# When ScalarE takes the side banks of a state-space scan, and a third buffer for turned values in attention

## The chip, the cores and the metric

The kernel runs on one core of one Trainium2 chip. A core has a matrix engine (TensorE, PE in the profile), a vector engine (VectorE, DVE), an activation engine (ScalarE, ACT), a general engine (GpSimd, POOL), and a sync engine (SyncE, SP) that here only issues DMAs. The metric is the device time of one execution in microseconds.

## The reference, cut to what matters

The input is `x` of 16 sequences x 1024 positions x 256. Three things are computed, each added to its input:

```
xz = layernorm(x) @ in_w.T;  x_, z = halves of xz (512 wide each)
u  = silu(conv4(x_) + conv_b)                        # causal, 4 taps
dt_in, B, C = u @ x_proj.T                           # 64, 16, 16 wide
delta = softplus(dt_in @ dt_w.T + dt_b)
h = h * exp(delta * A) + (delta * u) * B             # step by step, 512 channels x 16 states
y = (sum over states of h * C + u * D) * silu(z)
x = x + y @ out_w.T
n = layernorm(x)
attention over the 16 sequences at each place (16 heads of 16, causal),
then 8 experts of width 1024, two chosen per token, 320 x 16 rows at most each
x = x + n + attention + experts
```

All of it is float32.

## The kernel before, in words

There are four stages, one after the other: `mamba_stage` (state space), `attention_stage`, `routing_stage`, `expert_stage`. The change touches the first two. Every engine runs a list of its own, written out by hand; semaphores join the lists.

**State space.** The work is cut into 32 blocks: 16 sequences, each in two halves of 512 positions. A block is 32 units (`UNITS`): two passes over halves of the channels, each of 16 states. A unit has two chunks of 128 channels, so a block has 64 positions `v`, and position `v` belongs to unit `v // 2`. "Position" below always means this. Channels lie on the partitions and the 512 places along the row, so one VectorE instruction scans 128 channels of one state over 512 places.

For each position ScalarE makes `decay = exp(delta * A)` into one of two PSUM banks (L521). VectorE scans it (L639), which needs `decay` and GpSimd's `dbu = du * B` (L373). The decay of position `v` overwrites that of `v - 2`, so it waits for that scan. Per unit the state is multiplied by C: 13 of the 32 units (`POOL_UNITS`: remainder 1 or 3 by five) on GpSimd (L382), the other 19 on VectorE (L621, one scan later, with C spread over the partitions by a TensorE pick, L751). TensorE adds the products over the states with a unit matrix (`sum_unit`, L767). It does so two units later, for the first state of a pass three units later, after two products with the skip diagonal (L760). At positions 4 and 5 (second pass of the block before) and 36 and 37 (first pass) VectorE multiplies the finished sum by the gate (L575).

**The side work.** Beside scanning one block the kernel prepares the next one: turning the normed rows (`xnT`), the input projection (`x`), the convolution (`conv`), the B/C/dt projection (`dbl`), `dt`, and the gate branch (`z`). It also finishes the block before (`out`, the output projection). The list `SIDE` says at which position TensorE does which piece of 0.9 us or so. Three PSUM banks (`SIDE_BANKS`) take these uses in turn. The use at index n can be filled when the one at n - 3 has been emptied. Who empties a bank, and at which position after the last piece:

- `xnT`, `x`, `dbl`: one ScalarE copy, 1 position later (`take`, called from `prepare`);
- `dt`: ScalarE takes it 1 position later (two instructions), `softplus_exp` 2 later, `softplus_ln` 3 later, and VectorE adds the two parts of delta 4 later (L613);
- `conv` and `z`: ScalarE takes them 2 positions later (tanh, and for conv a scaled copy), VectorE's `silu` (L567) is 3 later;
- `out`: VectorE's `add_residual` (L581), 1 later.

`prepare` runs on ScalarE after the decay of its position; `finishing` and `preparation` run on VectorE after the scan of theirs. On TensorE the even piece of a unit comes before that unit's `sum_unit`, the odd piece after it, and the pick last. Each list is strict in its order, so an engine that waits in one of these steps holds everything behind it.

Derived places: `REST_AT`, `MIDDLE_AT` and `LOW_AT` split C into three bf16 parts (VectorE, ScalarE twice, VectorE); `STORE_ROWS_AT` is the unit at which SyncE stores the B and C rows; `DU_AT` are the two units at which GpSimd makes `du = delta * u` (`du_part`, L365) for the next block; `STATS_AT` and `NORMALISE_AT` place the statistics and the norm. The first block is prepared ahead of the loop. The last block prepares nothing.

**Attention.** 64 items of 16 places each pass through a pipeline of steps; the constants (`KDIAG`, `VTURN`, ...) say how many steps after its start an item reaches an operation. For an item VectorE turns the values into `vtr` (`turn_values`, L1225) at lag 10, GpSimd spreads them with 8 DMAs into the block-diagonal `vbd` (`place_values`, L1066) at lag 11, and TensorE multiplies by them at lag 13. `vtr` and `vbd` both have two buffers. VectorE's list of a step ends with `statistics`, `turn_values`, `statistics_2`; GpSimd's is `inverse_deviation_2`, `inverse_deviation`, `place_values`.

## Time and profile before

| | us |
|---|---|
| three runs | 7350.12, 7351.43, 7352.06 (median 7351.43) |
| profiled execution, whole | 7356.11 |
| profiled execution, span of the core | 7354.4 |
| busy: PE / DVE / ACT / POOL | 6352.4 / 4186.9 / 3217.9 / 5285.3 |
| share of the span | 86% / 57% / 44% / 72% |

The page's slices show three kinds of stretch. Up to about 4100 us (state space) PE, DVE and POOL are all at 8 or 9 tenths. From there to about 4950 us (attention) PE is at 9. After a short stretch in which nearly only POOL works (routing), the experts run from about 5300 us to the end with PE at 9 and the others low. The core's whole time is the sum of these stages, so what a change in a stage brings is read inside it.

### The profile page before, as it was taken

Reading aid. Unit: us, or ns where it says so; the run is one execution under the profiler, and the core shown is the slowest. Engines: PE = TensorE matmul, PEld = TensorE weight load, DVE = VectorE, ACT = ScalarE, POOL = GpSimd, SP = SyncE. Lnnn points to the kernel's source line nnn. Section 1 sums busy time; section 2 is a strip of 40 time slices with the busy share of each in tenths; the row PEclk is TensorE's granted clock in tenths of the full one; section 3 lists DMA queues with packets and bytes.
Section 4 is the critical chain, followed back from the end, with each engine's and each line's share of the span. In section 5 each row is a group of like instructions: output and inputs, shape, how many; then the busy total and the mean of one; then the engine's idle time right before and its main releaser. Section 6 shows DMA issues by size and latency. Waiting matters only on the chain. (4 is left out here: it accounts for less than half of the span.)

```text
span 7354.4 us, 88415 instructions
## 1 busy us (share of the span) xinstructions
PE 6352.4 (86%) x25412; PEld 3944.7 (54%) x25412; DVE 4186.9 (57%) x5063; ACT 3217.9 (44%) x5905; POOL 5285.3 (72%) x4089
## 2 busy tenths in 40 slices
PE   7989989898989989898888799970089999999999
PEld 3433434334434434343343577760078888888888
DVE  6988888888888888888888465661000000000000
ACT  5555555555555555555555466650022222222222
POOL 6988888888888888888889666636744444444444
PEclk9999999999999999999999999985599999999999
DMA  3333333333333333333333233330055555555554
GB/s 90 112 104 108 103 112 104 111 104 110 103 104 111 104 111 99 112 104 110 104 108 107 69 100 108 109 114 1 1 184 181 176 181 176 177 179 174 178 155 133
DMA packets 469314, 869.97 MB, mean 118 GB/s; under 512 B 72818, under 2 KB 241268, under 8 KB 434352
## 3 DMA queue, kind: packets, MB, share of 16 engines
q1 hardware_dynamic: 353616, 509.92, 23.2%
q0 software_dynamic: 115296, 355.56, 16.0%
q8 instruction: 147, 2.41, 0.1%
q14 instruction: 255, 2.09, 0.1%
HBM read 766.65 MB, written 88.88 MB: 116 GB/s over the span
## 5 line engine op out<-in xcount | busy, mean ns | idle before, releaser
L373 POOL TENSOR_TENSOR m_dbu<-m_du,m_bb 128x1024 f32<-128x1024 f32 x1024 | 2390.7, 2355 | 135.8 <-DVE m_h L639 135.2
L767 PE MATMUL m_y_bank<-m_prod,m_ident 128*128 128x512 f32 x4096 | 1995.0, 614 | 170.9 <-POOL m_prod L382 169.9
L521 ACT ACTIVATE m_decay<-m_delta,m_a_neg 128x512 f32<-128x512 f32 x2048 | 1402.8, 692 | 1121.9 <-DVE m_h L639 1112.9
L767 PEld LDWEIGHTS m_y_bank<-m_prod,m_ident 128*128 128x128 f32 x4096 | 787.0, 196 | 1163.9 <-issue 883.3
L639 DVE TENSOR_TENSOR_SCAN m_h<-m_decay,m_h_end,m_dbu 128x512 f32<-128x512 f32 x1024 | 1268.3, 1270 | 168.2 <-ACT m_decay L521 152.8
L639 DVE TENSOR_TENSOR_SCAN m_h<-m_decay,m_dbu 128x512 f32<-128x512 f32 x1024 | 1208.0, 1211 | 234.8 <-ACT m_decay L521 175.0
L1717 DVE TENSOR_SCALAR e_ye<-e_ybank,e_listing 128x256 f32<-128x256 f32 x270 | 118.3, 480 | 1887.1 <-PE e_ybank L1752 1887.1
L382 POOL TENSOR_TENSOR m_prod<-m_h,m_cb 128x1024 f32<-128x1024 f32 x416 | 978.5, 2352 | 247.2 <-DVE m_h L639 198.9
L1752 PE MATMUL e_ybank<-e_w,e_a 128*128 128x256 f32 x4320 | 968.5, 382 | 35.1 <-ACT e_a L1703 35.1
L1703 ACT ACTIVATE e_a<-e_ubank 128x512 f32<-128x512 f32 x540 | 322.4, 597 | 1543.4 <-PE e_ubank L1743 1541.1
L1743 PE MATMUL e_ubank<-e_xT,e_w 128*128 128x256 f32 x4320 | 956.0, 379 | 1.3 <-ACT e_xT L1694 1.3
L1752 PEld LDWEIGHTS e_ybank<-e_w,e_a 128*128 128x128 f32 x4320 | 809.6, 190 | 171.9 <-ACT e_a L1703 67.3
L1743 PEld LDWEIGHTS e_ubank<-e_xT,e_w 128*128 128x128 f32 x4320 | 821.8, 190 | 113.6 <-issue 1.6
L1647 POOL DMA_INDIRECT e_w<-in_w,weight_row x270 | 258.3, 957 | 847.3 <-PE e_ybank L1752 800.5
L621 DVE TENSOR_TENSOR m_prod<-m_h,m_c_bank 128x1024 f32<-128x1024 f32 x608 | 728.2, 1198 | 93.1 <-PE m_c_bank L751 79.4
L725 PE MATMUL m_side<-m_xnT,m_w_in 128*128 128x512 f32 x1024 | 546.8, 634 | 19.8 <-ACT m_xnT L440 19.8
L1664 POOL DMA_INDIRECT out<-e_ye,e_token x270 | 430.1, 1593 | 113.7 <-issue 81.3
L730 PE MATMUL m_side<-m_xpad,m_tap_diag 128*128 128x512 f32 x1024 | 505.8, 592 | 0.0
L1729 PE MATMUL e_tbank<-e_ident,e_xe 128*128 128x128 f32 x540 | 81.5, 274 | 368.4 <-DMA e_xe<-n,e_token 368.4
L751 PE MATMUL m_c_bank<-m_c_parts,m_pick 80*128 80x512 bf16 x608 | 239.2, 393 | 164.1 <-DVE m_prod L621 164.0
L1481 POOL DMA_INDIRECT info<-r_entry,r_slot_of x256 | 250.9, 980 | 134.7 <-issue 80.4
L1655 POOL DMA_INDIRECT e_xe<-n,e_token x270 | 284.1, 1052 | 82.5 <-issue 82.5
(207 smaller groups left out, 6705.5 us busy)
## 6 DMA issues: line engine op xcount, KB each, us to landing
m_bb<-rows_bc SPq DMA_DIRECT2D x1024, 256.0 KB, 3.5
m_cb<-rows_bc SPq DMA_DIRECT2D x416, 256.0 KB, 3.4
m_xin<-in_x SPq DMA_DIRECT2D x32, 512.0 KB, 5.3
m_xres<-in_x SPq DMA_DIRECT2D x32, 512.0 KB, 5.3
x<-m_xres SPq DMA_DIRECT2D x32, 512.0 KB, 4.9
a_xa<-x SPq DMA_DIRECT2D x64, 256.0 KB, 2.9
a_xr<-x SPq DMA_DIRECT2D x64, 256.0 KB, 3.1
out<-a_out_base SPq DMA_DIRECT2D x64, 256.0 KB, 3.1
```

Of the source, the lines that this page charges most:

```text
L373: nc.gpsimd.tensor_tensor(dbu[:, slot], du[:, q[1], p * PC:(p + 1) * PC], bb[:, slot].unsqueeze(1).to_broadcast([P, PC, T]), ALU.mult).the ...
L382: nc.gpsimd.tensor_tensor(prod[:, slot], h[:, slot], cb[:, C_BUFFER[k]].unsqueeze(1).to_broadcast([P, PC, T]), ALU.mult).then_inc(prod_by_ ...
L521: nc.scalar.activation(decay[:, cc], delta[:, r, c], ACT.Exp, scale=a_neg[:, c, n:n + 1]).then_inc(decay_done, 1)
L621: nc.vector.tensor_tensor(prod[:, slot], h[:, slot], c_bank[:].unsqueeze(1).to_broadcast([P, PC, T]), ALU.mult).then_inc(prod_by_vector, 1)
L639: nc.vector.tensor_tensor_scan(h[:, slot, cc], decay[:, cc], dbu[:, slot, cc], h_end[:, u, cc:cc + 1] if r else 0.0, ALU.mult, ALU.add).th ...
L725: ins = nc.tensor.matmul(bank, w_in[:, piece, col:col + P], xnT[:, piece], start=(piece == 0), stop=final)
L730: ins = nc.tensor.matmul(bank, tap_diag[:, i, piece], xpad[:, i, piece:piece + T], start=(piece == 0), stop=final)
L767: ins = nc.tensor.matmul(y_bank[:, cc], ident[:], prod[:, slot, cc], start=False, stop=(n == NS - 1))
L1664: nc.gpsimd.indirect_dma_start(out, bass.IndirectOffsetOnAxis(ap=token[:, col:col + 1], axis=0), ye[:, n % Y_RING, j], None, compute_op=AL ...
L1703: nc.scalar.activation(a[:, n % 2, g * PER_U:(g + 1) * PER_U], ubank[:, (n * UG + g) % U_RING], ACT.Gelu).then_inc(u_taken, 1)
L1743: ins = nc.tensor.matmul(ubank[:, (n * UG + g) % U_RING, i], w1[:, r, k, c * P:(c + 1) * P], xT[:, n % 2, k], start=(k == 0), stop=(k == K ...
L1752: ins = nc.tensor.matmul(ybank[:, n % 2, j], a[:, n % 2, c, j * P:(j + 1) * P], w2[:, r, c], start=(c == 0), stop=(c == FC - 1))
```

## The change

ScalarE's takes move from 1 to 3 positions after the last piece (`TAKE`), and from 2 to 4 for conv and z (`TAKE_SILU`). `softplus_exp` and `softplus_ln` move with them (to 4 and 5), VectorE's `silu` goes from 3 to 4 and delta from 4 to 5. In `SIDE` the x uses begin one position later, `dt` and `out` one later, `z` where it was, so a rest before `z` is gone. `MIDDLE_AT` is three positions after `REST_AT` and `LOW_AT` is at the same position as `MIDDLE_AT`. In attention `vtr` has three buffers, and `turn_values` waits for the placing of the item three before instead of two before.

```diff
-    SIDE = [("xnT", 0, 1), ("xnT", 1, 1), REST, ("x", 0, KH), ("x", 1, KH), REST, ("conv", 0, TAPS), ("x", 2, KH),
+    SIDE = [("xnT", 0, 1), ("xnT", 1, 1), REST, REST, ("x", 0, KH), ("x", 1, KH), ("conv", 0, TAPS), ("x", 2, KH),
             ("conv", 1, TAPS), ("x", 3, KH), ("conv", 2, TAPS), REST, ("conv", 3, TAPS), REST, REST, ("dbl", 0, CH),
-            REST, REST, ("dt", 0, 1), ("out", 0, 4), ("dt", 1, 1), ("out", 1, 4), ("dt", 2, 1), REST, ("dt", 3, 1),
-            REST, REST, ("z", 0, KH), ("z", 1, KH), ("z", 2, KH), ("z", 3, KH), REST, REST, REST, REST]
+            REST, REST, REST, ("dt", 0, 1), ("out", 0, 4), ("dt", 1, 1), ("out", 1, 4), ("dt", 2, 1), REST, ("dt", 3, 1),
+            REST, ("z", 0, KH), ("z", 1, KH), ("z", 2, KH), ("z", 3, KH), REST, REST, REST, REST]
+    TAKE, TAKE_SILU = 3, 4
...
-    assert position_of["z", CH - 1] + 3 < POSITIONS
+    assert position_of["z", CH - 1] + TAKE_SILU < POSITIONS
     STATS_AT = position_of["dt", 0] + 3
     NORMALISE_AT = STATS_AT + 8
-    REST_AT = position_of["dbl", 0] + 2
-    MIDDLE_AT = REST_AT + 1
-    LOW_AT = MIDDLE_AT + 1
-    STORE_ROWS_AT = (position_of["dbl", 0] + 2) // PC
-    DU_AT = ((position_of["dt", 1] + 4) // PC + 3, (position_of["dt", 3] + 4) // PC + 1)
+    REST_AT = position_of["dbl", 0] + TAKE
+    MIDDLE_AT = REST_AT + 3
+    LOW_AT = MIDDLE_AT
+    STORE_ROWS_AT = (position_of["dbl", 0] + 2 + TAKE) // PC
+    DU_AT = ((position_of["dt", 1] + TAKE + 2) // PC + 3, (position_of["dt", 3] + TAKE + 2) // PC + 1)
...
-                if v - 2 in filled_at and filled_at[v - 2][0] in SILU_KINDS:
-                    take(q, *filled_at[v - 2])
-                if v - 1 in filled_at and filled_at[v - 1] in prep_uses and filled_at[v - 1][0] not in SILU_KINDS:
-                    take(q, *filled_at[v - 1])
-                if v - 2 in filled_at and filled_at[v - 2][0] == "dt":
-                    softplus_exp(q, filled_at[v - 2][1])
-                if v - 3 in filled_at and filled_at[v - 3][0] == "dt":
-                    softplus_ln(q, filled_at[v - 3][1])
+                silu_of, plain = filled_at.get(v - TAKE_SILU), filled_at.get(v - TAKE)
+                exp_of, ln_of = filled_at.get(v - TAKE - 1), filled_at.get(v - TAKE - 2)
+                if silu_of and silu_of[0] in SILU_KINDS:
+                    take(q, *silu_of)
+                if plain in prep_uses and plain[0] not in SILU_KINDS:
+                    take(q, *plain)
+                if exp_of and exp_of[0] == "dt":
+                    softplus_exp(q, exp_of[1])
+                if ln_of and ln_of[0] == "dt":
+                    softplus_ln(q, ln_of[1])
...
-                if v - 3 in filled_at and filled_at[v - 3][0] in SILU_KINDS:
-                    silu(p, *filled_at[v - 3])
-                if v - 4 in filled_at and filled_at[v - 4][0] == "dt":
-                    c = filled_at[v - 4][1]
+                silu_of, dt_of = filled_at.get(v - TAKE_SILU), filled_at.get(v - TAKE - 2)
+                if silu_of and silu_of[0] in SILU_KINDS:
+                    silu(p, *silu_of)
+                if dt_of and dt_of[0] == "dt":
+                    c = dt_of[1]
...
-    X_RING, RES_RING, SIDE_BANKS = 4, 3, 4
+    X_RING, RES_RING, SIDE_BANKS, TURN_RING = 4, 3, 4, 3
...
-        vtr = sb("vtr", [P, 2, 2, GL, HD])
+        vtr = sb("vtr", [P, TURN_RING, 2, GL, HD])
...
-                    nc.gpsimd.dma_start(vbd[rows, k % 2, g], vtr[rows, k % 2, g % 2]).then_inc(v_placed[k % 2], 16)
+                    nc.gpsimd.dma_start(vbd[rows, k % 2, g], vtr[rows, k % TURN_RING, g % 2]).then_inc(v_placed[k % 2], 16)
...
-                wait(dve, v_placed[k % 2], turns(k - 2, 2, KV))
-                nc.vector.transpose(vtr[:, k % 2].rearrange("p g l d -> p l g d"),
+                if k >= TURN_RING:
+                    wait(dve, v_placed[(k - TURN_RING) % 2], turns(k - TURN_RING, 2, KV))
+                nc.vector.transpose(vtr[:, k % TURN_RING].rearrange("p g l d -> p l g d"),
```

By the lists, this is where some steps stand (position before, position after): take of `x` 0: 5, 8; of `dbl`: 35, 37; `rest`: 36, 37; `middle`: 37, 40; `low`: 38, 40; last piece of `dt` 0 to 3: 37, 42, 47, 49 before and 38, 43, 48, 50 after; take of `dt` 2: 48, 51; deltas 0 to 3: 41, 46, 51, 53 before and 43, 48, 53, 55 after; takes of `z` 0 to 3: 55, 57, 59, 61 before and 57, 59, 61, 63 after; `du_part`: units 26 and 27 before, 27 and 28 after. Between the emptying of a bank and the first piece of the next use there were at least 2 positions before; now it is 1 for `out` 1 (freed by delta 0 at 43, filled from 44), `z` 1 (53, 54), `z` 2 (55, 56) and `z` 3 (57, 58).

## Rows read from the trace of the kernel before

**Rows 1.** Windows: length, busy us (instructions) by engine, clock, DMA share, GB/s.

```profile
300.00:4000.00 3700.00, 3319.41 (x8030) 1474.42 (x8031) 3227.83 (x3243) 2029.16 (x3659) 3242.34 (x1492) 0.95 0.36 107
...
4250.00:4800.00 550.00, 508.89 (x5177) 431.63 (x5176) 332.53 (x787) 376.93 (x754) 348.67 (x935) 0.97 0.36 105
...
5400.00:7200.00 1800.00, 1769.49 (x8290) 1532.98 (x8289) 106.87 (x244) 401.92 (x732) 877.99 (x732) 1.00 0.57 175
```

**Rows 2.** Waits of DVE, 300 to 4200 us: total, times, longest.

```profile
DVE m_h L639 <- ACT m_decay L521: 310.9, 275, 3.3
DVE m_prod L621 <- PE m_c_bank L751: 79.4, 43, 5.9
DVE m_h L639 <- POOL m_prod L382: 34.7, 11, 4.1
```

**Rows 3.** Waits of ACT, the same stretch.

```profile
ACT m_sp_r L470 <- PE m_side L738: 172.5, 58, 4.8
ACT m_tanh L460 <- PE m_side L725: 165.1, 86, 4.9
ACT m_tanh L457 <- PE m_side L730: 100.7, 87, 3.9
...
ACT m_c_middle L500 <- DVE m_side L602: 97.6, 29, 3.4
```

**Rows 4.** Windows of two blocks: scan 6, gate 36, scan 44, next scan 6.

```profile
2097.84:2153.10 55.26, 53.30 (x127) 23.00 (x127) 48.81 (x47) 29.18 (x59) 50.65 (x23) 1.00 0.33 99
2153.10:2171.86 18.76, 17.05 (x43) 8.58 (x44) 16.13 (x24) 11.16 (x21) 11.44 (x6) 0.82 0.32 103
2171.86:2221.96 50.10, 41.89 (x107) 18.34 (x105) 43.80 (x43) 30.39 (x61) 46.42 (x24) 0.97 0.39 121
2221.96:2277.30 55.34, 53.34 (x127) 23.00 (x127) 50.76 (x45) 27.75 (x44) 52.56 (x24) 1.00 0.33 98
2277.30:2295.32 18.02, 16.96 (x42) 8.89 (x43) 16.44 (x24) 10.65 (x17) 11.41 (x5) 0.82 0.37 110
2295.32:2350.26 54.94, 44.15 (x107) 18.87 (x106) 44.63 (x43) 29.87 (x52) 48.73 (x25) 0.94 0.38 111
```

**Rows 5.** Two groups of DVE, whole run: busy us, mean ns, idle before.

```profile
L621 DVE TENSOR_TENSOR m_prod<-m_h,m_c_bank 128x1024 f32<-128x1024 f32 x608 | 728.2, 1198 | 93.1 <-PE m_c_bank L751 79.4 <-issue 12.4 <-DVE m_h L639 0.7
...
L613 DVE TENSOR_TENSOR m_delta<-m_side,m_sp_r 128x512 f32<-128x512 f32 x128 | 85.9, 671 | 7.9 <-ACT m_side L484 7.9
```

**Rows 6.** Timeline of POOL, second half of a block: start, us.

```profile
2295.48 2.36 POOL L382 TENSOR_TENSOR m_prod<-m_h,m_cb 128x1024 f32<-128x1024 f32 x1 [2.46 <-DVE m_h L639]
...
2311.00 2.35 POOL L373 TENSOR_TENSOR m_dbu<-m_du,m_bb 128x1024 f32<-128x1024 f32 x1
2316.78 2.35 POOL L365 TENSOR_TENSOR m_du<-m_delta,m_xc 128x1024 f32<-128x1024 f32 x1 [3.42 <-DVE m_delta L613]
...
2328.33 2.34 POOL L382 TENSOR_TENSOR m_prod<-m_h,m_cb 128x1024 f32<-128x1024 f32 x1
...
2338.26 2.35 POOL L382 TENSOR_TENSOR m_prod<-m_h,m_cb 128x1024 f32<-128x1024 f32 x1 [0.65 <-DVE m_h L639]
```

**Rows 7.** Timeline of DVE and PE, the same block and one before.

```profile
2192.91 2.33 DVE L639 TENSOR_TENSOR_SCAN m_h<-m_decay,m_dbu 128x512 f32<-128x512 f32 x2
...
2323.80 2.95 PE L767 MATMUL m_y_bank<-m_prod,m_ident 128*128 128x512 f32 x4 [2.86 <-POOL m_prod L382]
...
2341.24 3.45 DVE L639 TENSOR_TENSOR_SCAN m_h<-m_decay,m_dbu 128x512 f32<-128x512 f32 x3 [3.14 <-POOL m_prod L382]
```

**Rows 8.** Attention, steps 16 to 58 (42 steps): window.

```profile
4311.40:4825.60 514.20, 469.47 (x4813) 397.93 (x4812) 311.50 (x736) 345.46 (x696) 316.52 (x841) 0.97 0.36 106
```

**Rows 9.** Attention, waits of DVE, 4250 to 4860 us.

```profile
DVE a_vtr L1225 <- DMA a_vbd<-a_vtr: 216.1, 51, 7.8
```

**Rows 10.** Attention, timeline of one step.

```profile
4510.29 3.91 POOL L1066 DMA_DIRECT2D a_vbd<-a_vtr  x8 [0.32 <-POOL a_shift_n L1052]
...
4517.37 0.71 DVE L1225 STREAM_TRANSPOSE a_vtr<-a_vT 128x512 f32<-128x512 f32 x1 [6.08 <-DMA a_vbd<-a_vtr]
```

## The prediction

> **What bounds the kernel now.** I read the windows by stage first, then who waits for whom inside a stage, then windows and timelines of two neighbouring blocks, since the takes move by positions inside a block. The reader should see three stages with three limits. In the experts PE is busy 98% of the stretch and the change touches nothing there. In attention PE has 92 or 93%. In the state space PE, POOL and DVE stand at 90, 88 and 87% [rows 1]: none is the bound alone, each waits for the others in turn. So I look for which list ends last in which part of a block.
>
> DVE's largest wait there is for ScalarE's decay, 310.9 us in 275 pieces; the wait for the picked C comes far behind [rows 2]. ScalarE is busy for only 55% of the stretch [rows 1], so it isn't slow, it is held: its takes wait for PE (172.5, 165.1, 100.7 us) and its middle part of C for DVE (97.6 us) [rows 3]. A decay queued behind such a take comes late. That is what the change goes at. The question is what ends next where the decay no longer does.
>
> Cut a block at scan 6, gate 36 and scan 44, and the two blocks of [rows 4] give A = 55.26 and 55.34 us, B = 18.76 and 18.02, C = 50.10 and 54.94, together 252.42, or 126.2 per block. In A PE is busy for 53.3 of 55.3 us at a granted clock of 1.00 (2.4 GHz): A belongs to PE, whatever ScalarE does. In B the clock is 0.82, part of the time at the 1.2 GHz level, and PE and DVE each have some idle time. In C DVE has 6.3 and 10.3 us of idle time, PE 8 to 11, and POOL 3.7 to 6.2 [rows 4].
>
> **Part 1, the takes in A (gain 0.8 us per block).** The piece of dt 0 leaves A for B and the last piece of x 1, which stood ahead of the skip products, now comes after them. A piece is about 0.86 us at full clock, half of a sum's 1.9 less its tail [rows 7]. PE's unbroken stretch in A is 53.3 less the dt piece (1.1) plus 0.86, so 53.1 us. DVE can't come right behind: its product of unit 15 needs a pick that PE issues 6.4 us before the end of that stretch (two sums of 1.9 us less tail, three pieces, a pick), and from there it has its product (1.2, [rows 5]), a silu (0.7), four scans at 1.14 (two in 2.33 us, less the 1.2 of one, [rows 7]) and another product (1.1) to gate 36. That is 46.8 + 7.7 = 54.5 us against 55.3. The ends: 53.2 (PE alone) and 56 (a piece late by one).
>
> **Part 2, B (gain 2.0).** The wait of 3.4 us per block for the middle part goes: DVE makes `rest` at 37, and ScalarE asks for it at 40. The take of dt 0 moves from one to three positions behind PE. DVE's own work in B is 16.13 and 16.44 us [rows 4] and nothing else is later than it, so B comes to 16.4, against 18.4 on the mean. Ends: 0 (PE's skip products start no earlier) and 2.3.
>
> **Part 3, C (gain 3.8).** DVE's own work is 43.8 and 44.6 us [rows 4]; for both I take 44.7. What is late next is POOL. From the product of unit 21 (start 2295.48) to the end of that of unit 31 (2340.61) it has 45.1 us, of which 3.42 go to `du` waiting for delta 3 and 0.65 to a scan [rows 6]. In the new order the product of unit 26 comes ahead of the second `du`, so the wait for delta 3 (now two positions later, and `du` one unit later) is filled: 41.1 us of work without a break. DVE, without its stops, has 19 scans at 1.14, five products at 1.2 and seven short steps like the delta at 0.67 [rows 5, 7] from scan 44 to product 30: 32.4 us. PE picks C for that product behind the sum of unit 28, and POOL ends the product of unit 28 today at 2330.67, 35.2 us after that of unit 21 began [rows 6]; without the wait for delta 3 that is 31.8. A sum of 1.9 and a pick of 0.4 follow: 34.1, so DVE waits 1.7 us. The clock adds to it. After an idle time of 2.86 us PE needed 2.95 us for a sum instead of 1.9 [rows 7], and the new idle time in front of the sum of unit 28 is about as long; another sum after 2.4 us was not slowed, so I take 0.8 of a possible 1.7. C is then 44.7 + 1.7 + 0.8 = 47.2 for the first block. In the second the loop's turn adds the 3.1 us in front of its first scan [rows 7], which the view gives to POOL but which stands at every second block start; it stays: 50.3. The mean gain is (2.9 + 4.6)/2 = 3.8. Ends: 1.0 (the wait for the pick grows to 4) and 6.5 (all of DVE's idle time but the loop's turn).
>
> The Trainium skill speaks against this part. "TensorE: Matmul & The Clock Gate", section "HAM oscillation — how this bites in real kernels", says that a matmul loop which waits between its bursts is put back to half rate at each wait. The trace agrees for one such wait, 2.95 us for a sum behind 2.86 us of idleness. If it held at every block, C would lose the full 1.7 us, 0.9 more than I take, and the time would be 28 us higher.
>
> **Part 4, the banks (0, ends 0 and 8 us per block).** Four uses now have one position between the emptying and the first piece: out 1, z 1, z 2, z 3. By the sum of Part 3 PE comes to z 2 and z 3 after DVE's delta 3 and silu, with 0.4 us to spare or to wait; z 1 waits up to 0.3 us for delta 2. PE has idle time in C [rows 4], which hides these. If that cover were gone, each costs up to a position, 2 us. ScalarE's extra work at one position is 1.9 us at most (end of dt 2 and take of dt 3 at 53), against scans, a product and a delta on DVE; it doesn't hold the decay. SyncE's store of the rows comes a unit later and holds the load of B for unit 23, which POOL reads only after scan 39: nothing.
>
> Per block 0.8 + 2.0 + 3.8 = 6.6 us. 31 of the 32 blocks prepare a next one: 205 us.
>
> **Part 5, the third buffer (gain 38 us).** Steps of attention take 514.2/42 = 12.2 us [rows 8]. DVE waits 216 us for the DMAs that spread the turned values [rows 9]. That wait closes a loop one step long: turn, second statistics, POOL's two inverse deviations, eight DMA issues of 3.91 us together, landing 3.2 us after the last issue (4514.20 to 4517.37), turn again [rows 10]. It takes a whole step, and PE loses 514.2 - 469.5 = 44.7 us over these 42 steps [rows 8]. With three buffers the placing waited for is two steps old, the loop has a step to spare, and PE's own work remains: 11.2 us per step. Over some 50 steps the most to be had is 1.06 x 50 = 53 us; the least is 0, since PE has 91% without it. I take 0.75 of 1.06 per step, 38 us, because ScalarE's copies and the bank order also cost PE short waits.
>
> **Sum.** 7356.1 - 205 - 38 = 7113 for an execution like the profiled one. The median of the three runs lies 4.7 us below that execution, so 7108.
>
> **Rivals.** (a) All of DVE's wait for the decay comes back: POOL and PE follow at once. For it: DVE is idle for 5 to 6 us of A and 6 to 10 us of C [rows 4]. Against: PE fills A without a gap. 311 + 50 give 6995. (b) C is POOL's: the idle time of DVE there turns into waits for picks and for POOL, and only A and B gain. For it: POOL has 46.4 of 50.1 us in C [rows 4]. Against: it loses 3.4 us to `du` that the new order fills. 31 x 2.8 = 87, with half of attention 19: 7245. (c) Slower: the banks of Part 4. PE would reach out 1, z 1, z 2 and z 3 before DVE has freed them, each time wait a position, and carry the lag through the next A, where it has no slack. Four waits of 2 us are 8.0 against the gain of 6.6, 1.4 x 31 = 43 us more, with nothing gained in attention: 7394. It decides from the point where the four waits together pass 6.6 us. For it: one position of slack where there were two to three. Against: PE is behind DVE in these units by the sum of Part 3. (d) The change does nothing measurable, since ScalarE's held time moves to another wait of the same length: 7351.
>
> **How the numbers follow.** A measurement of this kernel tells 0.2% (15 us) from no change. Forecast 0.57 (7050 to 7190), (a) 0.10, (b) 0.22, (c) 0.07, (d) 0.04. Range: the upper end 7285 takes in (b) with nothing from attention (7264); the lower end 7000 the far ends of Parts 3 and 5 (2.7 x 31 = 84 and 15 us lower: 7009); (a), (c) and (d) are left out. Faster 0.90, same 0.03, slower 0.07.
>
> **What would show it.** ScalarE's waits for PE's side banks near nothing, and for `middle` gone. DVE's wait for the decay from 311 us to below 60, its wait for picks up from 79 to over 120. A about 54.5, B 16.4, C 47 to 50 us in windows cut in the same way. GpSimd's wait for delta 3 under 1 us. In attention no DVE wait for the placing, steps of 11.4 us. The prediction is wrong if DVE waits as long as before under another name, if C stays over 49 on the mean, or if PE waits for banks at z 1 to z 3.

## The result, and the profile after

The changed kernel takes 7055.84 us (median of four runs, 7053.51 to 7057.36) against 7350.89 (7350.12 to 7352.06) for the kernel before on the same chip: a ratio of 0.9598, 95% interval 0.9582 to 0.9615. Its profiled execution took 7057.36 us, with a span of 7055.6. The forecast was 7108 with a range of 7000 to 7285. The direction and the range held, and the mechanism in the main; the saving was 295 us where I had worked out 243.

The two profiled executions lie 299 us apart. Of these the state space gives 215 (its last instruction ends at 3887.8 instead of 4103.3 us) and attention 83 (755.9 instead of 839.0 us long). Routing and the experts did not move.

The windows by stage of the kernel after, with the columns of [rows 1]. The second lies wholly in attention.

```profile
300.00:3800.00 3500.00, 3241.02 (x8039) 1451.05 (x8038) 3216.62 (x3250) 2049.89 (x3665) 3242.93 (x1495) 0.97 0.37 113
4030.00:4500.00 470.00, 470.00 (x5077) 407.29 (x5072) 340.30 (x772) 378.23 (x735) 358.12 (x926) 1.00 0.42 121
5100.00:6900.00 1800.00, 1769.49 (x8290) 1533.07 (x8289) 106.84 (x244) 401.90 (x731) 878.19 (x731) 1.00 0.58 175
```

The same 8030 or so matmuls of the state space now fit into 3500 us instead of 3700 [rows 1]: PE, DVE and POOL stand at 93, 92 and 93%. In attention PE is busy for 470.00 of 470.00 us at a clock of 1.00. PE's time in the experts, 1769.49 us, is that of before to a hundredth.

The waits of DVE in the state space, 300 to 3900 us (total, times, longest), against [rows 2]:

```profile
DVE m_prod L625 <- PE m_c_bank L755: 180.8, 78, 5.6
DVE m_prod L625 <- issue: 47.2, 29, 4.6
```

The 310.9 us for ScalarE's decay are gone to the last one. What is late next is the pick of C, 180.8 instead of 79.4 us. Taken together, DVE stands idle for 283 of 3500 us where it stood for 472 of 3700 [rows 1], with the same work: of the 311 us removed some 120 came back under other names.

The waits of ScalarE, same stretch, against [rows 3]:

```profile
ACT m_decay L524 <- DVE m_h L643: 1401.3, 1356, 7.3
ACT m_xpad L453 <- PE m_side L729: 48.2, 58, 1.3
```

Three waits for PE (438 us together) and the one for the middle part of C (97.6) are gone; of those for the x uses 48.2 us stay. ScalarE now waits for DVE to free a decay's buffer, which is what an engine does that runs ahead.

Two neighbouring blocks in windows cut as in [rows 4], parts A, B and C of each; here the block with the longer C stands first:

```profile
2104.71:2159.66 54.95, 53.03 (x128) 23.18 (x127) 50.44 (x46) 28.86 (x47) 51.56 (x23) 1.00 0.34 103
2159.66:2177.99 18.33, 18.19 (x42) 8.68 (x42) 16.34 (x25) 9.62 (x15) 12.73 (x7) 0.81 0.30 97
2177.99:2225.34 47.35, 40.27 (x107) 17.84 (x106) 44.39 (x45) 30.19 (x51) 47.19 (x25) 1.00 0.41 128
2225.34:2279.50 54.16, 52.90 (x127) 23.17 (x127) 48.70 (x47) 30.35 (x63) 49.88 (x22) 1.00 0.34 104
2279.50:2295.67 16.17, 15.16 (x43) 7.63 (x43) 15.83 (x25) 10.20 (x19) 13.28 (x7) 1.00 0.34 112
2295.67:2342.33 46.66, 41.53 (x106) 18.36 (x105) 43.45 (x45) 30.89 (x59) 46.50 (x24) 0.96 0.43 130
```

In C POOL is busy for 47.19 of 47.35 and 46.50 of 46.66 us: it is the bound there now, without a gap. In the two B's the instructions are the same, and one takes 2.16 us longer than the other; its clock is 0.81.

Over 28 blocks cut at the same instructions the means are, in us (worked out from the trace; "even" and "odd" are the first and second block of a turn of the loop; the last row but one is the time in which PE's clock was granted at 1.2 GHz and not at 2.4):

| | before | forecast | after |
|---|---|---|---|
| A | 55.33 | 54.5 | 54.57 |
| B | 18.53 | 16.4 | 17.53 |
| C, even | 50.31 | 47.2 | 46.21 |
| C, odd | 54.86 | 50.3 | 48.02 |
| whole block | 126.45 | 119.7 | 119.21 |
| PE's clock at its half level, per block | 12.4 | - | 6.0 |
| one of 39 steps of attention | 12.54 | 11.4 | 10.85 |

The forecast had no term for the last row but one beyond 0.8 us in C. PE's clock is at the half level for 6.5 us less per block, which is 3.2 us of its work. How much of the 7.2 us gained per block comes by that isn't shown apart from the waits; but the four runs below whose state space is over 30 us longer than that of the kernel after, though they have part of the change (e6, e7, e9 and e11), have it at the half level for 7.6 to 11.8 us per block.

### The profile page after: what moved, and what is told of

The parts are those of the page before. It is cut to its first block and busy times, and to the rows that moved or that the text cites. A ratio compares the mean times of both kernels' runs of the same rounds, so it can differ in the third digit from the quotient of the medians.

```text
span 7055.6 us, 88414 instructions
## 1 busy us (share of the span) xinstructions
PE 6230.5 (88%) x25412; PEld 3901.4 (55%) x25412; DVE 4180.4 (59%) x5063; ACT 3247.7 (46%) x5905; POOL 5293.3 (75%) x4089
## 5 line engine op out<-in xcount | busy, mean ns | idle before, releaser
L771 PE MATMUL m_y_bank<-m_prod,m_ident 128*128 128x512 f32 x4096 | 1968.7, 608 | 158.1 <-POOL m_prod L383 157.5
L729 PE MATMUL m_side<-m_xnT,m_w_in 128*128 128x512 f32 x1024 | 521.9, 609 | 2.1 <-ACT m_xnT L441 0.7
L729 PEld LDWEIGHTS m_side<-m_xnT,m_w_in 128*128 128x128 f32 x1024 | 194.1, 194 | 236.3 <-issue 199.2
```

Of the source, the lines that this page charges most:

```text
L729: ins = nc.tensor.matmul(bank, w_in[:, piece, col:col + P], xnT[:, piece], start=(piece == 0), stop=final)
L771: ins = nc.tensor.matmul(y_bank[:, cc], ident[:], prod[:, slot, cc], start=False, stop=(n == NS - 1))
```

## The experiments

**My theory:** the two edits are independent and their gains add up. In the state space ScalarE stood in takes that waited for PE, and POOL in the second `du` before delta 3; in attention the closed loop of one step is the cause, not DVE's wait as such. **The rivals:** one of the parts (the takes, the place of `du`, the new side order) brings it all and the others are idle; the third buffer helps because DVE waits less.

### e1: the third buffer alone, in the kernel before

```diff
-        vtr = sb("vtr", [P, 2, 2, GL, HD])
+        vtr = sb("vtr", [P, TURN_RING, 2, GL, HD])      # TURN_RING = 3
-                wait(dve, v_placed[k % 2], turns(k - 2, 2, KV))
+                if k >= TURN_RING:
+                    wait(dve, v_placed[(k - TURN_RING) % 2], turns(k - TURN_RING, 2, KV))
```

> The kernel before with nothing but the third buffer for the turned values. Theory: the 83 us that attention lost between the two traces (839 to 756 us) belong to the ring alone, so this comes to 7351 - 83 = 7268 us, steps of 10.85 us and no half clock in them. Rival 1: the ring is worth the 38 us that I had forecast, and the rest came with the state space's new order (what it leaves in the queues at the stage's end): 7313. Rival 2: the two parts help each other, and alone each brings less than its share.

Measured: 7267.29 us (7264.19 to 7270.75), ratio 0.9889 [0.9872, 0.9905], 81 us less than the 7348.69 beside it. The steps take 10.85 us as in the kernel after. The gain of attention comes whole without the other edit.

### e2: the state space alone

```diff
-    X_RING, RES_RING, SIDE_BANKS, TURN_RING = 4, 3, 4, 3
+    X_RING, RES_RING, SIDE_BANKS, TURN_RING = 4, 3, 4, 2
```

> The changed kernel with two buffers for the turned values again, so the later takes and the new side order alone. Theory: the state space keeps its 215 us, attention goes back to steps of about 12.3 us: 7351 - 215 = 7136 us. Rival: part of the 215 is not of the takes; then it is above 7150.

Measured: 7142.61 us (7132.57 to 7144.45), ratio 0.9718 [0.9701, 0.9734], 206 us less. The state space ends at 3888.8 us, attention takes 839.8. And 81 + 206 = 287 against 295, within the 12 us by which the runs of e2 alone differ: the two edits add up.

### e3: two buffers, but the statistics ahead of the turn

DVE's list only: in a step the second statistics, for which POOL waits, are issued before the turn of the values and no longer behind it.

```diff
+                for k in items(step, STATS2):
+                    statistics_2(k)
                 for k in items(step, VTURN):
                     turn_values(k)
-                for k in items(step, STATS2):
-                    statistics_2(k)
```

> The kernel before, two buffers, with statistics_2 ahead of turn_values in VectorE's list. Theory (a loop through VectorE's order): what costs is not the wait for the placing itself, but that GpSimd's inverse deviations stand behind it through statistics_2. With statistics_2 ahead, the loop turn, next step's vector work (6.8 us), inverse deviations (4.7), placing (3.9), landing (3.2) takes 19.3 us and spans two steps, 9.7 us per step, under TensorE's 10.85. So steps go to 10.9 to 11.1 us and the time to 7268 to 7280, with two buffers only. Rival: two buffers are too few in any order, and the time stays within 10 us of 7351.

Measured: 7270.91 us (7268.56 to 7273.38), ratio 0.9894 [0.9878, 0.9911], 78 us less. The third buffer's gain comes without a third buffer. The waits of DVE in e3, 4250 to 4700 us:

```profile
DVE a_hid L1233 <- PE a_side L1360: 66.4, 37, 2.4
DVE a_vtr L1225 <- DMA a_vbd<-a_vtr: 50.0, 25, 5.3
```

DVE still waits for the placing, 50.0 us in 25 pieces, and that costs nothing: PE is busy for all of these 450 us. The wait of [rows 9] did harm only because the statistics stood behind it and POOL's placing behind the statistics. This settles it: the loop was the cause, the wait a sign of it.

### e4: four buffers instead of three

```diff
-    X_RING, RES_RING, SIDE_BANKS, TURN_RING = 4, 3, 4, 3
+    X_RING, RES_RING, SIDE_BANKS, TURN_RING = 4, 3, 4, 4
```

> The changed kernel with four buffers for the turned values. Theory: with three, TensorE is busy for 423.0 of 423.0 us over 39 steps and is the bound, so a fourth brings nothing: 7056, within 3 us. Rival: VectorE still loses something to the placing at some steps: 5 us or more less.

Measured: 7060.36 us (7058.99 to 7064.15), ratio 0.961 [0.9594, 0.9626]. No difference from the kernel after. A step is PE's now.

### e5: ScalarE asks for the middle part of C early again

```diff
-    MIDDLE_AT = REST_AT + 3
-    LOW_AT = MIDDLE_AT
+    MIDDLE_AT = REST_AT + 1
+    LOW_AT = MIDDLE_AT + 1
```

> The changed kernel with MIDDLE_AT one position after REST_AT and LOW_AT one later, so ScalarE again asks for VectorE's rest right behind it. Theory: ScalarE is held for about 2 to 3 us per block, but VectorE then has the scan of 38 to do; the decay of 39 is 0.7 us late, so 0.7 x 31 = 20 us: 7056 + 20 = 7076 at most, and 7056 if the wait for the pick at 42 (1.1 us) swallows it. Rival: ScalarE's wait counts in full, 3.4 us per block: 7160.

Measured: 7066.0 us (7060.19 to 7070.63), ratio 0.9611 [0.9595, 0.9627], 10 us more than the kernel after. The intervals of the two ratios overlap; the traces tell them apart: the state space ends at 3899 us, and at 3888 or 3889 in the three traces with the state space of the kernel after (that kernel, e2 and e4). The wait of ScalarE comes back, and then the wait of DVE behind it, in two views of e5:

```profile
ACT m_c_middle L503 <- DVE m_side L605: 81.2, 29, 2.9
...
DVE m_h L643 <- ACT m_decay L524: 15.9, 29, 0.6
```

ScalarE is held for 2.8 us each time, of which 0.55 reach DVE. With the takes in their new places ScalarE runs far enough ahead that a stop of this kind costs a fifth of itself: this edit is worth some 10 us of the 295, inside the 0 to 20 that I had worked out.

### e6: the takes moved, `du` at its old unit

```diff
-    DU_AT = ((position_of["dt", 1] + TAKE + 2) // PC + 3, (position_of["dt", 3] + TAKE + 2) // PC + 1)
+    DU_AT = ((position_of["dt", 1] + TAKE + 2) // PC + 2, (position_of["dt", 3] + TAKE + 2) // PC)
```

> The changed kernel with GpSimd's two du parts one unit earlier (26 and 27, as before the change), everything else as changed. Theory: GpSimd sets the pace of the second half of a block, and the changed kernel gained by filling its wait for delta 3 with the product of unit 26. Put back, du 1 would be ready to start 0.4 us before scan 54 and delta 3 ends 3.0 us after it: 3.4 us lost per block, 3.4 x 31 = 105 us: 7160, at least 7130. Rival: VectorE sets the pace there and GpSimd's wait is hidden: within 15 us of 7056.

Measured: 7213.73 us (7212.85 to 7214.2), ratio 0.9815 [0.9799, 0.9832], 158 us more than the kernel after. A and B stay (54.74 and 17.32 us), C goes from 47.11 to 52.38, almost back to the 52.59 of before. The waits in e6, one line each of POOL, ScalarE and DVE:

```profile
POOL m_du L366 <- DVE m_delta L617: 88.7, 28, 3.4
...
ACT m_tanh L461 <- PE m_side L729: 144.0, 58, 4.7
...
DVE m_h L643 <- POOL m_dbu L374: 84.8, 59, 4.5
```

POOL stands 3.2 us per block before delta 3. Its next updates come late, DVE's scans wait for those, its silus and with them PE's z pieces are late, and ScalarE waits at the tanh of z. Two `du` parts one unit too early cost 5.3 us per block, more than POOL's own wait of 3.2, which was all that I had priced (105 us). A part of the rest is the clock: PE's time at the half level in C goes from 2.3 to 8.8 us per block, and from a granted 1.00 in the kernel after, C of such an odd block goes to 0.91. The window of C in such a block of e6:

```profile
2262.22:2316.46 54.24, 44.09 (x107) 19.39 (x106) 44.67 (x45) 30.25 (x51) 47.87 (x25) 0.91 0.36 112
```

### e7: the takes two and three positions behind, not three and four

```diff
-    TAKE, TAKE_SILU = 3, 4
+    TAKE, TAKE_SILU = 2, 3
```

> The changed kernel with TAKE 2 and TAKE_SILU 3 (one position less each), in the new side order. Theory: TensorE's pieces end less than three positions behind their place, and where the take still waits VectorE has slack: within 15 us of 7056. Rival: each position of delay counts, and half of the gain in ScalarE's waits is lost: 7100 or more.

Measured: 7125.92 us (7122.91 to 7130.8), ratio 0.9695 [0.9679, 0.9712], 70 us more than the kernel after. My expectation failed, the rival's held. A stays at 54.58, B and C grow by 1.25 and 1.10 us. DVE waits for the decay again, 86.1 us in 58 pieces, at position 10 (2.4 us on the mean) and at 22 (0.6). At 10 the take of x 1 comes up while the last piece of x 1 still stands behind PE's skip products. That explains a wait in A, which A hides, since its end doesn't move. What B and C pay is in part the clock: PE's time at the half level goes from 3.7 to 5.1 us in B and from 2.3 to 3.8 in C. Why it does, the runs don't settle.

### e8: a shorter way to x, on top of the kernel after

The take of the normalized rows (`xnT`) moves to one position behind its filling, and x 0 and x 1 start a position earlier, as in the kernel before.

```diff
-    SIDE = [("xnT", 0, 1), ("xnT", 1, 1), REST, REST, ("x", 0, KH), ("x", 1, KH), ("conv", 0, TAPS), ("x", 2, KH),
+    SIDE = [("xnT", 0, 1), ("xnT", 1, 1), REST, ("x", 0, KH), ("x", 1, KH), REST, ("conv", 0, TAPS), ("x", 2, KH),
...
+                if filled_at.get(v - 1, REST)[0] == "xnT":
+                    take(q, *filled_at[v - 1])
```

> The changed kernel with the xnT banks taken one position after their filling again, and the two x uses a position earlier for it, as in the old order, so the last piece of x 1 stands ahead of the skip products again. Theory: part A of a block is TensorE's, 53.0 of 54.6 us busy at full clock, so a piece of 0.86 us less in it shortens every block by 0.8: 7056 - 25 = 7031. Rival: what A gives is lost to GpSimd, which has 94% of a block: within 8 us of 7056.

Measured: 7038.99 us (7027.19 to 7045.74), ratio 0.958 [0.9564, 0.9596], 17 us less than the kernel after. A falls by 0.80 to 53.77 us, as worked out: one piece of PE's unbroken list leaves A. The total fell by 17 us where I had worked out 25; the runs of e8 lie up to 19 us apart. In A PE's own list is the bound, though not to the end of A, as e10 shows.

### e9: `du` one unit later, alone, in the kernel before

```diff
-    DU_AT = ((position_of["dt", 1] + 4) // PC + 3, (position_of["dt", 3] + 4) // PC + 1)
+    DU_AT = ((position_of["dt", 1] + 4) // PC + 4, (position_of["dt", 3] + 4) // PC + 2)
```

> The kernel before with only the two du parts one unit later (27 and 28), so that the product of unit 26 stands ahead of the second. Theory: in the changed kernel the place of du was worth 158 us; part of it is that TensorE's sum of unit 26 comes 4.7 us sooner and lets z 2 and z 3 be filled, which is also what ScalarE's takes of z wait for in the kernel before (VectorE stops 2.5 us per block at position 60). So the place alone gives back that stop and GpSimd's 3.4 us in part: 2 to 3 us per block, 60 to 95 us: 7255 to 7290. Rival: without the later takes the place brings nothing, since the decays stay late: 7340 or more.

Measured: 7259.86 us (7252.56 to 7265.46), ratio 0.987 [0.9854, 0.9887], 91 us less than before. C falls from 52.59 to 49.24 us; the takes stay where they were. The waits of ScalarE and DVE in e9:

```profile
ACT m_tanh L460 <- PE m_side L725: 12.0, 32, 0.7
...
DVE m_h L639 <- ACT m_decay L521: 250.5, 245, 2.7
```

ScalarE's second largest wait for PE, 165.1 us in [rows 3], falls to 12.0, though no take was moved: it hung on POOL by way of DVE's silus and PE's z pieces. DVE still waits 250.5 us for the decay. So this is a second limit beside the takes. Now the account of the state space: `du` alone 91; the takes with the new order but the old `du` (e6, less the 81 of the buffer) 136 − 81 = 55; both 206. 60 us are to be had only by both together. In C the same is seen: −0.2 (e6), −3.4 (e9), −5.5 (both).

### e10: e8, with the pieces of `dbl` one position later

```diff
-    TAKE, TAKE_SILU = 3, 4
+    TAKE, TAKE_SILU, TAKE_DBL = 3, 4, 2
...
-    REST_AT = position_of["dbl", 0] + TAKE
+    REST_AT = position_of["dbl", 0] + TAKE_DBL
```

> A version to beat the changed kernel: the xnT banks taken one position behind as in the run before, the four pieces of dbl one position later (32 to 35) and taken two positions behind, so that its last piece falls behind TensorE's sum of unit 15. Theory: part A has another piece of 0.86 us less on TensorE; VectorE has 48.7 to 50.4 us of own work there, so A goes from 53.8 to 53.0: 7039 - 25 = 7014. Rival: the take of dbl now waits for TensorE and holds the decays at 37 and 38, and B loses what A gains: 7035 to 7045.

Measured: 7034.84 us (7027.45 to 7042.16), ratio 0.9564 [0.9548, 0.958]. Against e8 no difference, where I had worked out 25 us. The rival's number held, its reason didn't: B didn't lose what A gained, since A gained nothing (53.71 against 53.77 us, B 17.33 against 17.34). DVE's two longest stops in A, in a block of e8 and then in one of e10, ahead of the same two products (start, us, and in brackets the idle time before it):

```profile
1864.77 1.22 DVE L627 TENSOR_TENSOR m_prod<-m_h,m_c_bank 128x1024 f32<-128x1024 f32 x1 [2.02 <-PE m_c_bank L757]
...
1882.66 1.22 DVE L627 TENSOR_TENSOR m_prod<-m_h,m_c_bank 128x1024 f32<-128x1024 f32 x1 [1.44 <-issue]
```

```profile
2101.34 1.22 DVE L629 TENSOR_TENSOR m_prod<-m_h,m_c_bank 128x1024 f32<-128x1024 f32 x1 [2.04 <-PE m_c_bank L759]
...
2119.23 1.22 DVE L629 TENSOR_TENSOR m_prod<-m_h,m_c_bank 128x1024 f32<-128x1024 f32 x1 [1.44 <-issue]
```

The stops at positions 12 and 22 are the same in both. From position 22 on DVE runs on its own work to the gate. The piece that e8 takes out of A stood ahead of that stop (position 7 in the kernel after), the one of e10 behind it (position 34). Only what PE does before the last stop counts for the end of A.

### e11: the takes moved, the side order of the kernel before

```diff
-    SIDE = [("xnT", 0, 1), ("xnT", 1, 1), REST, REST, ("x", 0, KH), ("x", 1, KH), ("conv", 0, TAPS), ("x", 2, KH),
+    SIDE = [("xnT", 0, 1), ("xnT", 1, 1), REST, ("x", 0, KH), ("x", 1, KH), REST, ("conv", 0, TAPS), ("x", 2, KH),
...
+            REST, REST, ("dt", 0, 1), ("out", 0, 4), ("dt", 1, 1), ("out", 1, 4), ("dt", 2, 1), REST, ("dt", 3, 1),
+            REST, REST, ("z", 0, KH), ("z", 1, KH), ("z", 2, KH), ("z", 3, KH), REST, REST, REST, REST]
```

> The changed kernel's takes (3 and 4 positions) with the side order of before; rest, middle, du and store places follow from their formulas. Theory: the shift of the order isn't what gains. Part A is lighter by a piece as in e8, dt is filled a position earlier: 7025 to 7060. Rival: the shift is needed, since x 0 at position 3 has to wait for the xnT take at 4 and dt 0 at 37 for the dbl take at 37: 7080 or more.

Measured: 7100.38 us (7097.72 to 7105.5), ratio 0.9658 [0.9642, 0.9675], 45 us more than the kernel after. My expectation failed, the rival's held. The waits of PE in e11:

```profile
PE m_side L729 <- ACT m_xnT L441: 54.5, 27, 5.3
...
PE m_side L742 <- ACT m_dbl L467: 38.2, 29, 1.7
```

A take is somebody's input. `xnT` 1 is taken at position 4, three behind its filling, and x 0 is filled from position 3 on: PE comes to x 0 before its rows are there and stands for 2.0 us per block, with all sums of POOL's products behind it; C goes to 49.71 us. At dt 0 it stands for `dbl` in the same way, 1.3 us per block. The shift belongs to the takes: it makes room where a consumer followed too closely. e8 cures the same place from the other side.

### e12: e8, with two matmuls that nobody reads ahead of the gate

They go into the bank of dt 0 while it is free, at positions 36 and 37, and change no result.

```diff
+    WARM = (36, 37)
...
+                if v in WARM and preps:
+                    if v == WARM[0]:
+                        bank_free(q, ("dt", 0), outs, preps)
+                    nc.tensor.matmul(side_bank[:, bank_of("dt", 0)], ident[:], w_in[:, 0, 0:T], start=True, stop=True)
```

> The kernel of e8 with two matmuls more per block whose result nobody reads, at positions 36 and 37, where TensorE stands idle for 1.7 us ahead of the pick of unit 18 and 0.7 us ahead of the skip products. In the changed kernel part B of a block lasts 16.16 us in the 8 of 28 blocks in which the granted clock stayed at the full level, 17.6 with 3.4 us at the half level and 18.3 to 19 with 6.8 us. Theory: what B misses against the forecast (17.5 for 16.4) is the clock alone, which falls after that idle time. With it filled B is 16.2 in nearly every block, 1.2 x 31 = 37 us less than e8: 7002. Rival 1: the clock falls all the same, from the idle time before it, and the matmuls only hold up the pick: 7039 or more. Rival 2: B is shorter, but C, which GpSimd sets, gives it back: 7030 to 7040.

Measured: 7033.6 us (five runs, 7013.64 to 7042.49), ratio 0.9562 [0.9549, 0.9576], not to be told from e8. The 37 us that I had worked out didn't come; my second rival held. B itself does as expected: 16.39 us, at full clock in 27 of 28 blocks. Three windows of e12, B and C of an odd block and B of the next:

```profile
2155.80:2172.33 16.53, 15.34 (x43) 7.63 (x43) 16.24 (x25) 9.63 (x15) 12.75 (x7) 1.00 0.40 108
2172.33:2223.63 51.30, 44.04 (x107) 18.91 (x107) 44.39 (x45) 30.23 (x51) 47.79 (x25) 0.93 0.38 118
...
2276.93:2293.11 16.18, 15.58 (x45) 7.63 (x43) 15.84 (x25) 10.21 (x19) 13.30 (x7) 1.00 0.41 114
```

B of the odd block takes 16.53 us, where the kernel after has 18.33, and C gives it back: 51.30 us at a clock of 0.93, where the kernel after has 47.35 at 1.00. On the mean B is 0.95 shorter than in e8, C 0.85 and A 0.45 longer. PE's time at the half level falls from 3.1 to 0.1 us per block in B and grows from 2.4 to 4.9 in C; over the whole block it is 5.5 us in e8 and 5.4 in e12. Driven from one place, it turned up in another.

e8, e10 and e12 beat both kernels, at 7034 to 7039 us: some 17 to 22 us below the kernel after. Runs of one of these kernels lie up to 29 us apart, so their order among themselves stays open. Part of the spread goes with the clock: the fastest run of e12 (7013.64 us) has a mean granted clock of 0.960, the slowest (7042.49) one of 0.954.

## Why the prediction was right, and where its sizes were off

**Part 1 (A): the sum right, its reason not.** 54.57 us against 54.5. I had DVE bound by the pick of unit 15. Its timeline in the kernel after, from position 12 of the block of the windows above:

```profile
2118.47 1.22 DVE L625 TENSOR_TENSOR m_prod<-m_h,m_c_bank 128x1024 f32<-128x1024 f32 x1 [2.88 <-PE m_c_bank L755]
...
2136.36 1.22 DVE L625 TENSOR_TENSOR m_prod<-m_h,m_c_bank 128x1024 f32<-128x1024 f32 x1 [1.44 <-issue]
...
2174.48 1.22 DVE L625 TENSOR_TENSOR m_prod<-m_h,m_c_bank 128x1024 f32<-128x1024 f32 x1 [1.70 <-PE m_c_bank L755]
```

The last stop in A is at position 22, at 2136.36. The view puts it down to "issue"; the pick that this product needs ends at 2136.26, and in the even blocks the same stop is given to the pick. From there the gate comes 23.3 us later on DVE's work alone, and the next stop is in B. The pick that binds is that of a unit long before. Where I placed it I took PE's stretch of 53.1 us and counted back from its end; the right way is to look for the last stop in front of the cut and count forward. The two differ by little here, because both lists are nearly full; that the sum fits to 0.1 us is luck.

**Part 2 (B): the wait went, the clock took half of the gain.** B was to be 16.4 and is 17.53 us. The bound itself was right: in the 8 of 28 blocks without half rate in B it is 16.16 us. In the other 20 it is 18.07. PE's timeline around the gate in the block with the longer B:

```profile
2155.87 1.88 PE L771 MATMUL m_y_bank<-m_prod,m_ident 128*128 128x512 f32 x4
2159.80 0.39 PE L755 MATMUL m_c_bank<-m_c_parts,m_pick 80*128 80x512 bf16 x1 [2.06 <-DVE m_prod L625]
2160.12 2.07 PE L742 MATMUL m_side<-m_dbl,m_w_dt 64*128 64x512 f32 x2
2162.17 3.78 PE L764 MATMUL m_y_bank<-m_xc,m_skip_diag 128*128 128x512 f32 x4
2165.74 4.17 PE L771 MATMUL m_y_bank<-m_prod,m_ident 128*128 128x512 f32 x8
...
2276.49 1.88 PE L771 MATMUL m_y_bank<-m_prod,m_ident 128*128 128x512 f32 x4
2279.64 0.39 PE L755 MATMUL m_c_bank<-m_c_parts,m_pick 80*128 80x512 bf16 x1 [1.27 <-DVE m_prod L625]
2279.96 1.12 PE L742 MATMUL m_side<-m_dbl,m_w_dt 64*128 64x512 f32 x2
2281.95 1.98 PE L764 MATMUL m_y_bank<-m_xc,m_skip_diag 128*128 128x512 f32 x4 [0.87 <-DVE m_zs L578]
2283.77 3.60 PE L771 MATMUL m_y_bank<-m_prod,m_ident 128*128 128x512 f32 x8
```

After an idle time of 2.06 us the same instructions took 2.07, 3.78 and 4.17 us, after 1.27 and 0.87 us they took 1.12, 1.98 and 3.60: 3.3 us of PE's time, at the 1.2 GHz level where the other is at 2.4. I had the clock of 0.82 in B before me [rows 4] and didn't price it: I let B fall to DVE's own work, as if the half rate would go with ScalarE's wait. It follows PE's stop at the pick ahead of the gate, which waits for DVE's product, and the edit leaves that stop. The stop of 2.06 us was followed by half rate in all 14 odd blocks, those of 1.27 and 0.87 us in 6 of the 14 even ones. e12, which fills the stop, is the proof for B. The term was 1.1 us too good, 35 us over 31 blocks.

**Part 3 (C): the mechanism as said, better than its size.** From the product of unit 21 to the end of that of unit 31 POOL now takes 41.0 us; I had 41.1. Its timeline in the kernel after, against [rows 6]:

```profile
2177.12 2.35 POOL L383 TENSOR_TENSOR m_prod<-m_h,m_cb 128x1024 f32<-128x1024 f32 x1 [5.03 <-PE m_y_bank L771]
...
2197.30 2.36 POOL L383 TENSOR_TENSOR m_prod<-m_h,m_cb 128x1024 f32<-128x1024 f32 x1
2199.61 2.35 POOL L366 TENSOR_TENSOR m_du<-m_delta,m_xc 128x1024 f32<-128x1024 f32 x1
...
2206.55 2.34 POOL L383 TENSOR_TENSOR m_prod<-m_h,m_cb 128x1024 f32<-128x1024 f32 x1
```

The product of unit 26 (2197.30) stands ahead of the second `du` (2199.61), and neither waits. e6 and e9 show both halves of it: without the move C is 52.4, with the move alone 49.2. Together C is 47.11 us on the mean where I had 48.75, which is 51 us over 31 blocks and more than pays for B. Three sizes were too dear.

The first is DVE's own work, which I took at 44.7 us for both blocks: it is 43.5 in the even ones and 44.4 in the odd ones. That is more than the whole error in the even blocks (46.21 us for 47.2).

The second is the clock. The stop in front of the sum of unit 28 came, in all 28 blocks and with 2.74 to 2.78 us in each. PE's timeline at that sum, in an odd block and in the even one after it:

```profile
2208.95 1.98 PE L771 MATMUL m_y_bank<-m_prod,m_ident 128*128 128x512 f32 x4 [2.75 <-POOL m_prod L383]
...
2326.56 3.07 PE L771 MATMUL m_y_bank<-m_prod,m_ident 128*128 128x512 f32 x4 [2.75 <-POOL m_prod L383]
```

The same 2.75 us of idleness, and then 1.98 us for the sum or 3.07. In 18 of the 28 blocks it took 1.98 us, in 10 between 2.40 and 3.44, which is 0.36 us on the mean of all where I had added 0.8. So a stop's length alone doesn't decide, and no row of mine showed the 1.7 us that I called possible; the nearest, C of the first block in [rows 4], has 1.5 us by its clock of 0.97. The page of the Trainium skill that I had weighed ("TensorE: Matmul & The Clock Gate", section "HAM oscillation — how this bites in real kernels") describes waits longer than this stop, so it is neither borne out nor contradicted by this sum.

The third is the turn of the loop, which I had added at its full 3.1 us. DVE's timeline ahead of product 30 and at that turn in the odd block, and ahead of product 30 in the even one:

```profile
2211.59 1.22 DVE L625 TENSOR_TENSOR m_prod<-m_h,m_c_bank 128x1024 f32<-128x1024 f32 x1 [1.01 <-DVE m_h L643]
...
2216.31 3.45 DVE L643 TENSOR_TENSOR_SCAN m_h<-m_decay,m_dbu 128x512 f32<-128x512 f32 x3 [1.72 <-POOL m_dbu L374]
...
2330.09 1.22 DVE L625 TENSOR_TENSOR m_prod<-m_h,m_c_bank 128x1024 f32<-128x1024 f32 x1 [2.68 <-PE m_c_bank L755]
```

The wait for the pick, 1.7 us in my sum, is 1.0 in the odd block and 1.3 in even ones with a full-rate sum before it; the 2.68 shown stands behind the slow sum of 3.07. The turn takes 1.5 to 2.3 us in 10 of the 14 odd blocks. In three others, where PE ran at half rate in C for over 6 us, it takes 3.5 to 3.7, and there C is 50.6 to 50.8 us, near my 50.3; in the 11 without half rate it is 47.3. So the 3.1 us are no fixed price. What sets them stays open.

**Part 4 (banks): nothing, as said.** PE has no wait for a bank at z 1 to z 3. The rival (c), slower by the banks, is out; (b) was right in that C is POOL's, and wrong in its price. Rival (a), all of the decay's wait coming back, is out in the state space, 215 of 311 us; that the whole comes to 295 of its 361 is attention's doing.

**Part 5 (attention): 83 us where I had 38** (0.75 of 1.06 us over 50 steps is 40; the 38 is a slip). Two sizes failed. My stretch of 42 steps [rows 8] ended in shorter ones; the first 39 of them, in the kernel before and then after:

```profile
4311.40:4800.40 489.00, 448.21 (x4527) 380.05 (x4527) 293.38 (x698) 330.72 (x667) 304.66 (x816) 0.97 0.36 105
```

```profile
4094.30:4517.30 423.00, 423.00 (x4525) 367.40 (x4524) 305.79 (x696) 338.52 (x662) 316.32 (x810) 1.00 0.41 121
```

That is 12.54 and 10.85 us per step. And I took PE's busy time, 448.21 us or 11.5 per step, for its own work and the rest for all there was to win. But the same matmuls take 423.0 us when nothing stops them. PE ran at half rate for 31 of the 489 us, worth about 15 of the 25 us; the rest I can only argue. Behind a stop a group takes a tenth of a us more (1.98 for 1.88 in the timelines above), and PE stops 98 times in these steps, which would be the missing 10. And I discounted the gain to three quarters for short waits of PE, of which none came. With 1.69 us per step over 39 steps, 66 us, and 17 us in the others, this is the 83. The condition for no wait at the turn is met just so:

```profile
4207.02 3.91 POOL L1070 DMA_DIRECT2D a_vbd<-a_vtr  x8 [0.32 <-POOL a_shift_n L1056]
4210.96 0.68 DVE L1230 STREAM_TRANSPOSE a_vtr<-a_vT 128x512 f32<-128x512 f32 x1
```

The turn starts 0.03 us after the last of the eight issues, 3.2 us before a placing like that of [rows 10] would have landed; it writes a third buffer and needn't wait.

**The sum.** Forecast: 205 in the state space, 38 in attention. Measured: 215 and 83 between the traces. B was too good by 35 and C too dear by 51, A even: that is 16 for the 10 us missing, since the first and last blocks gain less than the mean. That the state space came so near is in part luck, two errors of opposite sign. Nearly the whole error of the forecast, 45 of its 52 us, is attention.

## What to carry to other kernels

When engines work in lists that wait for one another, look for the place where two lists are late at once: here one cure gave 91 us, the other 55, and both 206, so a cure tried alone and found small isn't yet refuted. A long wait is worth what stands behind it: 216 us for the placing cost attention 80, and with two instructions exchanged (e3) 50 us of the same wait cost nothing. And the busy time of an engine that is stopped again and again is no floor: price the gain by a stretch in which it is never stopped.

## What the runs showed of the hardware

TensorE's half rate after a stop is not a matter of that stop's length alone. In the kernel after, PE stands idle for 2.74 to 2.78 us ahead of the sum of unit 28 in each of 28 blocks; in 18 of them the sum then takes 1.98 us, in 10 between 2.40 and 3.44. A shorter stop, 2.06 us ahead of the gate, was followed by half rate in 14 of 14 blocks. Filling that stop with idle matmuls (e12 against e8) took PE's time at the half level from 3.1 to 0.1 us per block in B and from 2.4 to 4.9 in C, for no gain in time. And the stop at the turn of the loop, which I took for a fixed price of 3.1 us, was 1.5 to 2.3 us in 10 of 14 turns of the kernel after and 3.5 to 3.7 in three; what it consists of stays open.
